# A recommendation kernel: thirteen products of TensorE that nobody reads, added in the tail

## The chip, the cores and the metric

The kernel runs on one core of one Trainium2 chip. The metric is the device time of one execution in microseconds (us), the median over several executions. "TensorE" is the matrix engine (PE in the profile; its weight loads stand apart as PEld), VectorE is DVE, ScalarE is ACT, GpSimd is POOL and SyncE is SP.

## The reference

For each of 2048 samples the model takes 13 dense features and 26 indices, one for each embedding table of 12500 rows of 64 numbers:

```
x = relu(dense @ Wb0 + bb0)            # 13 -> 512
x = relu(x @ Wb1 + bb1)                # 512 -> 256
d = relu(x @ Wb2 + bb2)                # 256 -> 64
sp = emb[arange(26)[None, :], sparse_idx]
T = concatenate([sp, d[:, None, :]], axis=1)      # 27 vectors of 64
Z = einsum('bnd,bmd->bnm', T, T)                  # all their dot products
h = concatenate([d, Z below the diagonal], axis=1)   # 64 + 351
h = relu(h @ Wt0 + bt0)                # 415 -> 512
h = relu(h @ Wt1 + bt1)                # 512 -> 256
p = sigmoid(h @ Wt2 + bt2)             # 256 -> 1
```

Everything is fp32.

## The kernel before, in words

The batch is cut into eight steps of 256 samples, each of two units of 128. GpSimd gathers the embedding rows, 128 at a time, with indirect DMAs (L356, and L383 for the last ones). It is given about 50 such DMAs a step and issues them one behind another for the whole kernel. SyncE and ScalarE fetch the rows of the last table with small direct DMAs. TensorE turns the gathered rows (L422; in the last step L438), VectorE, in the last step ScalarE too, spreads them into `vecs_st`, TensorE makes the dot products (`gram`), VectorE transposes them by 32x32 blocks, ScalarE and VectorE pack the 351 pairs, TensorE turns those and runs the top layers.

The last step differs, since nothing follows that could hide its work. Its first half of the samples is gathered and multiplied ahead (`gram_last`, L484). Of the second half, tables 16 to 23 are gathered last of all, with eight DMAs (L383) into `rows`, in such an order that each quarter of the half can be finished as soon as its rows are there: quarters 0, 1 and 2 wait for two DMAs each, quarter 3 for two that are waited for one by one. TensorE's program runs in the order it is written in, and the only waits are semaphores. For each quarter q it holds:

- `turn_late(q)` (L451): a wait for the DMAs of the quarter and for the bank `ps_turn` to be free, and two transposes of 128x128 (for quarter 3 two calls with one each). ScalarE (L686) takes the turned rows of quarters 0 and 2 and of the last tile, VectorE (L831) those of quarter 1 and of the first tile of quarter 3. Each copies 64x128 once for each tile.
Behind quarter 3, VectorE transposes the sums (L846, L848), ScalarE and VectorE pack them (L692, L837), TensorE turns three tiles of pairs (`turn_feat_last`, L514 and L519; a transpose is one record), ScalarE and VectorE move them (L696, L841), TensorE adds twelve products of 117x128 by 128 columns to the two banks of the first top layer (`top_0_last`, L532, 24 records), ScalarE and VectorE take the relu of one half each (L720, L867), TensorE makes the second top layer (`top_1_sum`, L580, four products of 256 columns, eight records), VectorE the logits (L873), ScalarE the sigmoid (L771), SyncE stores.

The bank `ps_feat[1]` holds four blocks of 128 columns. In this stretch only its blocks 0 and 1 are used, and only from `turn_feat_last` on. `wt1_sb` holds the weights of the second top layer and is in place since the start.

Of the kernel before, what the change touches and what calls it, by code (L numbers as in the profile page):

```python
# [36 lines left out]
P = 128  # L37
# [79 lines left out]
def build(nc, x, idx, fetch_idx, emb, wb0, bb0, wb1, bb1, wb2, bb2, wt0, wt1, bt1, wt2, bt2, out):  # L117
# [3 lines left out]
    with ExitStack() as ctx:  # L121
        def sb(name, shape, dt=F32):
            return ctx.enter_context(nc.sbuf_tensor(name, shape, dt))

        def ps(name, shape):
            return ctx.enter_context(nc.psum_tensor(name, shape, F32))
# [9 lines left out]
        wt1_sb = sb("wt1_sb", [P, T0 // P, T1])  # L136
# [38 lines left out]
        ps_feat = [ps(f"ps_feat{u}", [P, 4, P]) for u in range(2)]  # L175
# [90 lines left out]
        def late_rows(q, k):  # L266

            return rows[:, LATE + LATE_TILES * q + k, :]
# [118 lines left out]
        def _(pe):  # L387
# [37 lines left out]
            def turn_last(k):  # L425

                h, r = LAST_RUNS[k]
                first, n = RUNS[r]
                pe.wait_ge(rows_landed_last[h][r], 16 * GATHERED[r])
                if r == NR - 1:  # L430
                    pe.wait_ge(fetched_moved, STEPS)
                if k >= 2 and k % 2 == 0:
                    pe.wait_ge(vecs_act, k // 2)
                if k >= 2 and k % 2 == 1:
                    pe.wait_ge(vecs_dve, (STEPS - 1) * NR + k // 2)
                cols = DIM * (h + 1)
                for j in range(n):
                    turned = nc.tensor.transpose(ps_turn[k % 2][0:cols, j, :], rows[:, first + j, 0:cols], ident[:, :])  # L438
                turned.then_inc(rows_turned, 1)

            def turn_late(l):

                q, tile, n = LATE_RUNS[l]
                k = LAST_NR + l
                pe.wait_ge(late_landed[l], 16 * n)
                if k % 2 == 0:
                    pe.wait_ge(vecs_act, k // 2)
                else:
                    pe.wait_ge(vecs_dve, (STEPS - 1) * NR + k // 2)
                for j in range(n):  # L450
                    turned = nc.tensor.transpose(ps_turn[k % 2][:, j, :], late_rows(q, tile + j), ident[:, :])  # L451
                turned.then_inc(rows_turned, 1)
# [20 lines left out]
            def gram_last():  # L473

                i = STEPS - 1

                pe.wait_ge(vecs_act, (NR + 1) // 2)
                pe.wait_ge(vecs_dve, i * NR + NR // 2)
                pe.wait_ge(d_placed, STEPS)
                for u in range(2):  # L480
                    for g in range(HALF):
                        for v in range(4):
                            c = 64 * u + 16 * v + g
                            summed = nc.tensor.matmul(  # L484
                                ps_gram[32 * v:32 * v + 32, u, g * VECS:(g + 1) * VECS],
                                vecs_st[0:DIM, c, :], vecs_st[0:DIM, c, 0:VECS],
                                start=True, stop=True, tile_position=(0, 32 * v))
                summed.then_inc(gram_summed, 1)

            def gram_quarter(q):  # L490

                if q == 0:
                    pe.wait_ge(gram_turned, (STEPS - 1) * 4 + 2)

                done = LAST_NR + (q + 1 if q < QUARTERS - 1 else len(LATE_RUNS))
                pe.wait_ge(vecs_act, (done + 1) // 2)
                pe.wait_ge(vecs_dve, (STEPS - 1) * NR + done // 2)
                part = slice(DIM, 2 * DIM)
                u = q // 2
                for g in range(8 * (q % 2), 8 * (q % 2) + 8):  # L500
                    for v in range(4):
                        c = 64 * u + 16 * v + g
                        summed = nc.tensor.matmul(  # L503
                            ps_gram[32 * v:32 * v + 32, u, g * VECS:(g + 1) * VECS],
                            vecs_st[part, c, :], vecs_st[part, c, 0:VECS],
                            start=True, stop=True, tile_position=(DIM, 32 * v))
                if q == QUARTERS - 1:
                    summed.then_inc(gram_summed, 1)

            def turn_feat_last():  # L510

                pe.wait_ge(feat_packed, STEPS * 2)
                for k in range(PAIR_TILES - 1):
                    turned = nc.tensor.transpose(ps_feat[1][0:PAIR_ROWS, k, :], feat[:, 1, k * PAIR_ROWS:(k + 1) * PAIR_ROWS],  # L514
                                                 ident[:, :])
                turned.then_inc(feat_turned, 1)

                pe.wait_ge(last_tile_packed, 1)
                nc.tensor.transpose(ps_turn[1][0:PAIR_ROWS, 0, :], feat[:, 1, (PAIR_TILES - 1) * PAIR_ROWS:],  # L519
                                    ident[:, :]).then_inc(last_tile_turned, 1)  # L520
# [16 lines left out]
            def turn_feat(i, u):  # L537

                pe.wait_ge(feat_packed, i * 2 + u + 1)
                for k in range(PAIR_TILES):  # L540
                    turned = nc.tensor.transpose(ps_feat[u][0:PAIR_ROWS, k, :],  # L541
                                                 feat[:, u, k * PAIR_ROWS:(k + 1) * PAIR_ROWS], ident[:, :])
                turned.then_inc(feat_turned, 1)

            def top_0(i, u, blocks=range(T0 // P)):

                for m in blocks:
                    if m == 0 and u == 0:
                        pe.wait_ge(d_copied, i + 1)
                    if m == 0 and u == 1:  # L550

                        pe.wait_ge(t0_low, i * 2 + 1)
                    nc.tensor.matmul(top_0_blocks(u, m // 2)[:, m % 2, :], wt0_sb[0:D_ROWS, PAIR_TILES, m * P:(m + 1) * P],  # L553
                                     d_t[:, u, :], start=True, stop=False)
                    if m == 0:

                        pe.wait_ge(feat_moved, i * 2 + u + 1)
                    for k in range(PAIR_TILES):
                        summed = nc.tensor.matmul(top_0_blocks(u, m // 2)[:, m % 2, :],  # L559
                                                  wt0_sb[0:PAIR_ROWS, k, m * P:(m + 1) * P],  # L560
                                                  feat_t[:, u, k, :], start=False, stop=(k == PAIR_TILES - 1))
                    if m % 2 == 1:
                        summed.then_inc(t0_summed, 1)
# [41 lines left out]
            def land(i, turn_run):  # L605

                turn_run(0)
                top_0(i - 1, 0)
                turn_run(1)
                turn_run(2)  # L610
                top_1(i - 1, 0)
                top_0(i - 1, 1)
                turn_run(3)
                turn_run(4)
                top_1(i - 1, 1)
                turn_run(5)
                turn_run(6)
# [8 lines left out]
            def last_step():  # L626
                i = STEPS - 1
                land(i, turn_last)
                gram_last()
                turn_last(7)  # L630
                turn_last(8)
                turn_feat(i, 0)
                top_0(i, 0, blocks=range(0, 2))
                turn_last(9)
                top_0(i, 0, blocks=range(2, 4))
                top_1_bias(i, 0)
                turn_last(10)
                top_1_sum(i, 0)
                turn_last(11)
                top_1_bias(i, 1)  # L640
                for m in range(T0 // P):
                    top_0_d_last(m)
                for q in range(QUARTERS):
                    turn_late(q)
                    if q == QUARTERS - 1:
                        turn_late(q + 1)
                    gram_quarter(q)
                turn_feat_last()

                pe.wait_ge(feat_moved, STEPS * 2)  # L650
                for k in range(PAIR_TILES - 1):
                    for m in range(T0 // P):
                        top_0_last(k, m)
                pe.wait_ge(last_tile_moved, 1)
                for m in range(T0 // P):
                    top_0_last(PAIR_TILES - 1, m)
                top_1_sum(i, 1)
# [8 lines left out]
            with pe.Fori(1, STEPS - 1) as i:  # L666
                step(i)
            last_step()

        @block.scalar  # L670
# [376 lines left out]
```

## Time and profile before

| what | value |
|---|---|
| median of 3 executions | 524.86 us (524.68 to 525.59) |
| the profiled execution, its own time | 525.79 us |
| its span, from the first to the last instruction | 524.0 us |
| granted TensorE clock, mean over the span | 0.72 |
| busy: PE, PEld, DVE, ACT, POOL | 307.0, 224.5, 243.9, 13.9, 380.6 us |

The rows below come from one profiled execution. Times in them are microseconds from the start of the span. The granted clock (PEclk) is a share of full speed: 1.00 is 2.4 GHz and 0.50 is 1.2 GHz; in between means that it changed within the stretch. Busy time of PE counts a matmul from its start to its modelled end, and matmuls overlap, so the busy mean of one record is longer than the distance from one record's start to the next.

### The profile page before, as it was taken

To read this page: it belongs to the slowest core of one execution; us is meant where nothing else is said; L and a number is where in the kernel's file an instruction comes from. 1 tells how busy PE (TensorE), PEld (TensorE's weight loads), DVE (VectorE), ACT (ScalarE), POOL (GpSimd) and SP (SyncE) were. 2 spreads that over 40 slices of the span, in tenths; PEclk is the share of its full clock that TensorE was granted. 3 is DMA by queue.
4 is the path that set the end of the run, shared out by engine and by line. 5 is a ranking of instruction groups with operands and counts; after the bars stand their busy time and mean duration, and the time that the engine had idled before them with its cause. 6 is when DMAs were issued, how large, how long until landed. Compare 5 with 4: busy or idle time off the path is not lost.

```text
span 524.0 us, 11950 instructions
## 1 busy us (share of the span) xinstructions
PE 307.0 (59%) x3370; PEld 224.5 (43%) x3370; DVE 243.9 (47%) x372; ACT 13.9 (3%) x26; POOL 380.6 (73%) x406
## 2 busy tenths in 40 slices
PE   4799983754474355442556723637437255487876
PEld 1233432742373234332346612626226253486755
DVE  6434866672574245622357334543447432632222
ACT  1000000000000000000000000000000000021211
POOL 5777777777777777777777777777777777777750
PEclk9978996795576755857567766676668675788576
DMA  6444323433244332444334443353324443332310
GB/s 204 38 27 28 29 30 28 29 29 30 29 29 28 27 30 28 28 27 29 26 29 27 29 27 30 26 29 28 28 29 28 28 28 28 26 27 28 28 24 2
DMA packets 19961, 16.84 MB, mean 32 GB/s; under 512 B 11683, under 2 KB 12972, under 8 KB 19897
## 3 DMA queue, kind: packets, MB, share of 16 engines
q0 software_dynamic: 12800, 13.13, 31.4%
q1 hardware_dynamic: 4378, 2.68, 3.3%
q10 hardware_dynamic: 2732, 0.51, 2.2%
q14 instruction: 39, 0.32, 0.3%
q8 instruction: 12, 0.20, 0.1%
HBM read 16.28 MB, written 0.01 MB: 31 GB/s over the span
## 4 chain that ended last, share of the span: by engine, by line
POOL 62%; issue 22%; PE 11%; DMA 3%; DVE 2%; ACT 0%; POOLq 0%; DVEq 0%; ACTq 0%
POOL rows L356 61%; PE ps_t L400 3%; DMA rows<-in_emb,idx_row 2%; PE ps_turn L408 1%; PE ps_t L580 1%; POOL rows L383 1%; PE ps_feat L391 1%; PE ps_gram L391 1%; DMA idx_raw<-in_idx 1%; PE ps_t L532 1%; DVE hb L779 1%; PE ps_turn L422 1%; PE ps_feat L532 0%; PE ps_gram L503 0%; PE ps_t L559 0%
## 5 line engine op out<-in xcount | busy, mean ns | idle before, releaser
L356 POOL DMA_INDIRECT rows<-in_emb,idx_row x392 | 371.4, 948 | 122.8 <-issue 118.9
L422 PE MATMUL ps_turn<-ident,rows 128*128 128x128 f32 x182 | 40.1, 359 | 145.8 <-DMA rows<-in_emb,idx_row 137.3
L821 DVE COPY vecs_st<-ps_turn 128x512 f32<-128x512 f32 (+1 forms) x49 | 46.9, 957 | 113.0 <-PE ps_turn L422 112.5
L821 DVE COPY vecs_mv<-ps_turn 64x512 f32<-64x512 f32 (+1 forms) x98 | 96.3, 982 | 0.7
L422 PEld LDWEIGHTS ps_turn<-ident,rows 128*128 128x128 f32 x182 | 26.1, 179 | 159.8 <-issue 150.0
L467 PE MATMUL ps_gram<-vecs_mv,vecs_st 128*32 128x54 f32 x1792 | 41.0, 278 | 29.1 <-DVE vecs_mv L821 15.6
L467 PEld LDWEIGHTS ps_gram<-vecs_mv,vecs_st 128*32 128x32 f32 x1792 | 37.6, 159 | 34.0 <-DVE vecs_mv L821 18.4
L580 PE MATMUL ps_t<-wt_sb,ht_t 128*128 128x256 f32 x128 | 51.2, 569 | 0.0
L580 PEld LDWEIGHTS ps_t<-wt_sb,ht_t 128*128 128x128 f32 x128 | 35.0, 286 | 14.9 <-issue 8.1
L846 DVE STREAM_TRANSPOSE gram_s<-ps_gram 128x864 f32<-128x864 f32 x16 | 17.3, 1083 | 48.0 <-PE ps_gram L467 36.9
L559 PE MATMUL ps_t<-feat_t,wt_sb 117*128 117x128 f32 x180 | 34.1, 342 | 0.2 <-ACT feat_t L714 0.2
L400 PE MATMUL ps_t<-hb,wb_sb 128*128 128x512 f32 x64 | 31.7, 654 | 3.6 <-DVE hb L779 3.6
L559 PEld LDWEIGHTS ps_t<-feat_t,wt_sb 117*128 117x128 f32 x180 | 32.2, 262 | 0.4 <-ACT feat_t L714 0.4
L559 PE MATMUL ps_feat<-feat_t,wt_sb 117*128 117x128 f32 x180 | 25.9, 282 | 0.0
L559 PEld LDWEIGHTS ps_feat<-feat_t,wt_sb 117*128 117x128 f32 x180 | 23.6, 200 | 0.0
L400 PEld LDWEIGHTS ps_t<-hb,wb_sb 128*128 128x128 f32 x64 | 13.3, 214 | 22.2 <-issue 17.0
L541 PE MATMUL ps_feat<-ident,feat 128*117 128x128 f32 x45 | 10.7, 356 | 17.4 <-DVE feat L854 16.3
L873 DVE SCALAR_TENSOR_TENSOR ht_w<-ps_t,wt_sb 128x256 f32<-128x256 f32 x16 | 6.8, 424 | 27.8 <-PE ps_t L580 27.7
L681 ACT ACTIVATE vecs_st<-ps_turn 64x512 f32<-64x512 f32 (+1 forms) x6 | 5.8, 962 | 466.7 <-PE ps_turn L438 466.7
L570 PE MATMUL ps_t<-bt_sb,ones 1*128 1x256 f32 x32 | 16.9, 621 | 0.1
L553 PE MATMUL ps_t<-d_t,wt_sb 65*128 65x128 f32 x60 | 16.3, 367 | 0.0
L541 PEld LDWEIGHTS ps_feat<-ident,feat 128*117 128x117 f32 x45 | 7.2, 218 | 20.1 <-DVE feat L854 17.8
(78 smaller groups left out, 240.9 us busy)
## 6 DMA issues: line engine op xcount, KB each, us to landing
fetched<-in_emb SPq DMA_DIRECT2D x1024, 0.2 KB
fetched<-in_emb ACTq DMA_DIRECT2D x1024, 0.2 KB
rows<-in_emb,idx_row POOLq DMA_INDIRECT x400, 3.3
wt_sb<-in_wt SPq DMA_DIRECT2D x1, 1024.0 KB
wb_sb<-in_wb SPq DMA_DIRECT2D x1, 512.0 KB
wt_sb<-in_wt SPq DMA_DIRECT2D x1, 512.0 KB
idx_raw<-in_idx SPq DMA_DIRECT2D x1, 179.0 KB, 3.0
wt_sb<-in_wt ACTq DMA_DIRECT2D x1, 128.0 KB
```

The lines of the kernel that those rows point to most:

```text
L356: nc.gpsimd.indirect_dma_start(rows[:, t, h * DIM:(h + 1) * DIM], None, emb_rows, bass.IndirectOffsetOnAxis(idx_row[:, c:c + 1], 0)).then_ ...
L391: nc.tensor.matmul(ps_b0[m], wb0_sb[:, m * P:(m + 1) * P], x_t[:, bass.ds(c * CHUNK, CHUNK)], start=True, stop=True).then_inc(b0_summed, 1)
L400: summed = nc.tensor.matmul((ps_t0, ps_t1)[m][:, :], wb1_sb[:, k, m * P:(m + 1) * P], hb0[:, k, :], start=(k == 0), stop=(k == B0 // P - 1))
L422: turned = nc.tensor.transpose(ps_turn[r % 2][:, j, :], rows[:, first + j, :], ident[:, :])
L467: summed = nc.tensor.matmul(ps_gram[32 * v:32 * v + 32, b, g * 2 * VECS:(g + 1) * 2 * VECS], vecs_st[:, c, :], vecs_mv[:, c, :, :].rearran ...
L541: turned = nc.tensor.transpose(ps_feat[u][0:PAIR_ROWS, k, :], feat[:, u, k * PAIR_ROWS:(k + 1) * PAIR_ROWS], ident[:, :])
L553: nc.tensor.matmul(top_0_blocks(u, m // 2)[:, m % 2, :], wt0_sb[0:D_ROWS, PAIR_TILES, m * P:(m + 1) * P], d_t[:, u, :], start=True, stop=F ...
L559: summed = nc.tensor.matmul(top_0_blocks(u, m // 2)[:, m % 2, :], wt0_sb[0:PAIR_ROWS, k, m * P:(m + 1) * P], feat_t[:, u, k, :], start=Fal ...
L570: nc.tensor.matmul(ps_t1[:, 0:T1], ones[0:1, :], bt1_sb[:, :], start=True, stop=False)
L580: summed = nc.tensor.matmul(ps_t1[:, 0:T1], ht0_t[:, k, :], wt1_sb[:, k, :], start=False, stop=(k == T0 // P - 1))
L821: moved = nc.vector.tensor_copy(to, source)
L846: nc.vector.transpose(gram_s[u][:, 0:VECS * SLOTS], unit_products(VECS)).then_inc(gram_turned, 1)
```

## The change

A helper `stay_busy(n)` issues n products: 128x128 of `wt1_sb` as weights, 256 columns of `wt1_sb` as the moving operand, into blocks 2 and 3 of `ps_feat[1]`. They wait for no semaphore and count up none, and no instruction reads what they write. In each quarter of the last half 2, 2, 2 and 1 of them stand between `turn_late` and `gram_quarter`, and 0, 1, 1 and 4 behind `gram_quarter`: 13 in all. No other engine's program is touched.

```diff
                 if q == QUARTERS - 1:
                     summed.then_inc(gram_summed, 1)
 
+            def stay_busy(n):
+
+                for _ in range(n):
+                    nc.tensor.matmul(ps_feat[1][:, 2:4, :].rearrange("p a c -> p (a c)"), wt1_sb[:, 0, 0:P], wt1_sb[:, 0, :],
+                                     start=True, stop=True)
+
             def turn_feat_last():
...
                     turn_late(q)
                     if q == QUARTERS - 1:
                         turn_late(q + 1)
+                    stay_busy((2, 2, 2, 1)[q])
                     gram_quarter(q)
+                    stay_busy((0, 1, 1, 4)[q])
                 turn_feat_last()
```

## Rows read from the trace of the kernel before

**Rows 1.** The page's chain that ended last, by engine, share of the span.

```profile
POOL 62%; issue 22%; PE 11%; DMA 3%; DVE 2%; ACT 0%; POOLq 0%; DVEq 0%; ACTq 0%
```

**Rows 2.** The chain of waits in order of time, from 500 us on: start, length, what.

```profile
503.10 2.76 DMA rows<-in_emb,idx_row
...
505.90 0.70 PE ps_turn L451 x2
...
507.27 1.07 PE ps_gram L503 x64
508.34 0.63 PE ps_turn L451 x2
...
509.43 1.12 PE ps_gram L503 x64
...
510.57 1.08 DVE gram_s L846
...
512.87 0.79 PE ps_feat L514 x2
...
514.12 1.23 PE ps_t L532 x4
515.34 0.85 PE ps_feat L532 x4
...
519.40 1.84 PE ps_t L580 x8
```

**Rows 3.** Busy time by stretch: us, busy (records) per engine, clock, DMA share, GB/s.

```profile
495.10:498.50 3.40, 3.40 (x22) 2.84 (x22) 0.42 (x1) 0.85 (x1) 2.48 (x4) 0.99 0.37 25
498.50:501.90 3.40, 3.30 (x20) 2.25 (x19) 1.46 (x3) 0.20 (x1) 2.48 (x4) 1.00 0.14 28
501.90:505.30 3.40, 1.91 (x130) 1.60 (x130) 0.59 (x2) 0.59 (x2) 2.78 (x3) 1.00 0.16 34
505.40:508.80 3.40, 2.27 (x73) 1.52 (x68) 0.02 (x1) 0.59 (x2) 0.95 (x1) 0.50 0.12 24
508.80:512.20 3.40, 1.23 (x65) 0.95 (x64) 1.96 (x4) 0.40 (x2) 0.00 (x0) 0.50 0.00 0
515.60:519.00 3.40, 3.40 (x18) 3.40 (x18) 0.00 (x0) 0.21 (x1) 0.00 (x0) 0.50 0.02 5
519.10:522.10 3.00, 2.12 (x11) 1.55 (x9) 0.86 (x3) 0.39 (x2) 0.00 (x0) 1.00 0.00 0
```

**Rows 4.** The timeline of the quarters: start, length, engine, line, operation, idle before.

```profile
503.50 0.44 PE L451 MATMUL ps_turn<-ident,rows 128*128 128x128 f32 x2
504.71 0.74 PE L503 MATMUL ps_gram<-vecs_st 64*32 64x27 f32 x64 [0.77 <-DVE vecs_st L831]
505.60 0.95 POOL L383 DMA_INDIRECT rows<-in_emb,idx_row  x1 [0.31 <-issue]
506.62 0.59 ACT L686 ACTIVATE vecs_st<-ps_turn 64x128 f32<-64x128 f32 x2 [4.12 <-PE ps_turn L451]
508.27 0.69 PE L451 MATMUL ps_turn<-ident,rows 128*128 128x128 f32 x2
509.43 1.07 PE L503 MATMUL ps_gram<-vecs_st 64*32 64x27 f32 x64 [0.47 <-ACT vecs_st L686]
518.79 0.38 ACT L720 ACTIVATE ht_t<-ps_t 128x256 f32<-128x256 f32 x1 [4.73 <-PE ps_t L532]
```

**Rows 5.** The timeline of TensorE: the same forms in steps before.

```profile
439.53 3.78 PE L580 MATMUL ps_t<-wt_sb,ht_t 128*128 128x256 f32 x8
...
469.80 0.39 PE L553 MATMUL ps_t<-d_t,wt_sb 65*128 65x128 f32 x2
...
473.37 1.04 PE L438 MATMUL ps_turn<-ident,rows 128*64 128x128 f32 x8
```

**Rows 6.** The timeline of TensorE in `gram_last`, whose records issue without pause.

```profile
481.88 2.16 PE L484 MATMUL ps_gram<-vecs_st 64*32 64x27 f32 x128 [1.42 <-issue]
...
485.34 0.33 PE L484 MATMUL ps_gram<-vecs_st 64*32 64x27 f32 x9 [1.30 <-issue]
```

## The prediction

> **What bounds the kernel now.** I read the chain that ended last first. GpSimd, which issues the gathers one behind another, holds 62% of it, and "issue" another 22%, most of it the pauses between those gathers [rows 1]. The change touches nothing that GpSimd waits for in its last step: the eight last gathers wait for no turned row that is still to come. So the kernel up to the last gather, issued at 505.60 [rows 4], stays as it is, and only what follows can move.
>
> Next I read the chain in order of time. From the landing of quarter 2's rows at 505.86 (the gather issued at 503.10 plus 2.76) the chain lies on TensorE and on what VectorE and ScalarE do between its pieces, up to the end [rows 2]. This tail takes 16 us, and the matmul pieces of it are the long ones.
>
> Then the clock, by stretch. TensorE has the full clock, 2.4 GHz, from 495.1 to 505.3, and 1.2 GHz from 505.4 to 519.0; it is back at 2.4 GHz for the last layer [rows 3]. What did the engine do before each change? From 495.1 to 501.9 it ran products of 128 and 256 columns nearly without pause, busy 3.40 and 3.30 of 3.40 us, and kept its clock. From 501.9 to 505.3 it was busy 1.91 of 3.40 us, and of its 130 records 128 were the small products of 64x32 by 27 columns; the clock was gone at the end of this. It came back after 515.6 to 519.0, busy 3.40 of 3.40 us with large products. So the tail does most of its large work at half speed because it was thin before. The added products are large and stand in that thin stretch.
>
> **The change, part by part.** All of it is TensorE's own program, no queue of a DMA is passed, and no wait is added. Behind each added product stand TensorE's own next instructions and whoever waits for them.
>
> The price of one product. Four products of 256 columns take 1.84 us at full clock [rows 2] and 3.78 at half [rows 5], so 0.46 and 0.95 us each. Thirteen cost 6.0 us of TensorE at full clock.
>
> Quarters 0 and 1. At 501.9 the clock is full. Two products are 0.92 us, and between the end of the transposes and the dot products TensorE idles 0.77 us for VectorE's copies [rows 4]; since matmuls are pipelined the products begin up to 0.2 us before the transposes' end, so each quarter is delayed by 0 to 0.15 us. The product behind quarter 1 (0.46 us) starts near 505.45 and ends near 505.9. Quarter 2 waits for the landing at 505.86 anyway [rows 2]. Cost: nothing, or 0.1 us; I take 0. If this cover were gone, the 0.15 us would come to stand on the path.
>
> Quarter 2. At full clock its transposes take 0.44 instead of 0.70 us and its dot products 0.74 instead of 1.07 [rows 2, 4]. With two products before them and one behind: 505.90, turned at 506.34, copies (0.59 us [rows 4]) to about 506.97, products to 507.0 or 507.2, dot products to 507.9, one more product to 508.3. Before, TensorE came to quarter 3 at 508.27 [rows 4]. The last gather, issued at 505.60, lands at 508.36 if it takes 2.76 us like the one of rows 2, and not after 508.5, since the second transpose of quarter 3 was then under way. What the clock gives here is thus used up by the added products and by this landing. Value 0, bounds 0.2 us either way.
>
> Quarter 3. The transposes are 0.69 us at half clock and 0.44 at full [rows 4], and as TensorE can do the first while the second tile is still landing, 0.25 to 0.42 us are gained; I take 0.35. The one product before the dot products (0.46 us) lies beside the copy, where TensorE idled 0.47 us [rows 4]: 0. The dot products take 0.74 instead of 1.07: 0.33 gained. Together 0.68.
>
> The four products behind quarter 3. They take 1.84 us at full clock. From the end of the dot products (509.43 + 1.12 = 510.55) to `turn_feat_last` at 512.87 are 2.32 us, in which VectorE transposes and ScalarE packs [rows 2]. Nothing is late, with 0.48 us to spare. At half clock they would take 3.78 and be 1.46 late.
>
> `turn_feat_last`. Two transposes and their drain: 0.79 us at half clock [rows 2]. At full clock the nearest row is the 0.44 of L451, two transposes also [rows 4]. Gained 0.35.
>
> `top_0_last`. At half clock four records advance by 0.85 us [rows 2]. At full clock the nearest are the 32 records of the same kind between 469.80 and 473.37 [rows 5], 3.57 / 32 = 0.112 us each. ScalarE can take the relu once 20 of the 24 are through: 518.79 - 514.12 = 4.67 us before [rows 2, 4], and 20 x 0.112 + 0.28 for the last record to end (the 0.39 of two records at 469.80 less 0.112 [rows 5]) = 2.52 after. The last four (0.45 us) lie beside that relu, as they did. Gained 2.15.
>
> The second top layer and what follows had the full clock already: 0.
>
> The sum is 0.68 + 0.35 + 2.15 = 3.18 us. Against the profiled execution's own 525.79 that gives 522.61, and I say **522.6 us**. The median of the runs shown is 0.93 us under the profiled execution, which is also above the highest of the three. I read the difference as the clock's: where in the tail it falls and rises is not tied to an instruction, and other executions can lose it later or get it back earlier. If the kernel no longer loses it, this spread goes and all executions should lie near 522.6. So the median should fall by about 2.3 us, not 3.2. About 0.2% (1 us) is what a measurement of this kernel can tell from no change.
>
> A rule that speaks against this. The rows say that the clock fell in a stretch in which TensorE never idled 0.8 us at a time but did small work [rows 3, 4]. The Trainium skill (TensorE: Matmul & The Clock Gate, "HAM oscillation — how this bites in real kernels") puts the loss down to idle gaps between bursts of matmuls. Read strictly, it finds no such gap here ahead of 505.4, and then filling the pauses would be no cure. The sum by it would be that of the first rival below; the trace, with the clock gone after pauses under 0.8 us, doesn't bear it out.
>
> **The rivals.** First, slower: the products don't hold the clock. It could fall for the kind of work (small tiles whatever stands between them), or because the chip takes it back after a time. Then each product costs 0.95 us. In quarter 2, two of them (1.90) against 0.68 us of cover cost 1.2, and the one behind it 0.95 more; in quarter 3 one against 0.47 costs 0.5; the last four cost 1.46: 4.1 us, thus 529.9. If the last four bring the clock up for `top_0_last`, 2.2 and some come back, and it is 527.5. It decides at 505.4: full clock there, and this rival is dead. For it speaks that no row shows added large products between these small ones; against it that 128 of 130 records before the fall were small, and that every stretch filled with large products kept or raised the clock [rows 3].
> Second, no change: the clock holds through the quarters but falls once between 509 and 513, where TensorE has the waits for the copies, 64 small products, and the pause before `turn_feat_last`. Then only quarter 3's 0.68 us is gained and the twelve products still run at half: 525.1 by the profiled execution, 0.2 over the median. Against it speaks that five products (2.3 us) now stand in this stretch, which had 1.23 of 3.40 us [rows 3].
>
> Third, a smaller gain: TensorE runs short of instructions. In `gram_last` it stood still for 1.42 and 1.30 us with nothing to wait for [rows 6], where 128 and more records issue without a pause. The change adds 26 records and their weight loads, and moves the places where more must be supplied. One such stop on the path gives 522.6 + 1.4 = 524.0. Against it: the added instructions are slow ones (0.23 us a record), and stops like this stand only in rows of small products.
>
> **How the numbers follow.** Forecast 80%, with its own range 521.8 to 523.3: the bounds above (0.2 either way in quarter 2, 0.15 in quarter 3, 0.3 for another last landing) and what another execution may add. Third rival 6%, second 8%, first 6%. To hold the time 8 times in 10 the range reaches from 521.7 to just over the third rival, 524.1. Faster by over 0.2%: forecast and third rival, 86%. Within 0.2%: the second, 8%. Slower: the first, 6%.
>
> **What would show it.** In the profile after: granted clock 1.00 in every stretch from 502 to the end; 64 records of the last quarter in 0.74 us, the 24 records of `top_0_last` in about 2.7 us, TensorE idle about 0.5 us before `turn_feat_last`, the dot products of quarter 2 beginning at 507.0 to 507.2, the landing of the last gather as the last wait on a DMA; executions closer together than the 0.9 us of before. A clock of 0.50 anywhere behind 505, or dot products that begin behind the copies by more than 0.3 us, would show me wrong.

## The result, and the profile after

The changed kernel takes 521.42 us, median of 4 executions (521.22 to 521.95), against 524.94 us for the kernel before (4 executions): a ratio of 0.9939, interval 0.9926 to 0.9952. That is 3.5 us less, where I forecast 2.3. The direction was right, but the time is 0.3 us under the low end of my range, 521.7. Measured again later (run again_c below), the same kernel took 522.09 us against 524.93, a ratio of 0.995 (0.9931 to 0.9968), 2.8 us less and within the range.

Busy time by stretch in the changed kernel, columns as in [rows 3] (microseconds busy and number of records for PE, PEld, DVE, ACT and POOL, then the granted clock):

```profile
498.50:501.90 3.40, 3.33 (x81) 2.53 (x80) 0.83 (x1) 0.61 (x2) 2.49 (x4) 1.00 0.14 29
501.90:505.30 3.40, 3.38 (x77) 2.72 (x78) 0.60 (x2) 0.40 (x2) 2.77 (x3) 1.00 0.18 34
505.40:508.80 3.40, 3.37 (x138) 2.51 (x137) 0.66 (x2) 0.48 (x2) 0.00 (x0) 1.00 0.06 14
508.80:512.20 3.40, 2.61 (x14) 1.88 (x13) 1.85 (x4) 1.02 (x2) 0.00 (x0) 1.00 0.02 5
512.20:514.70 2.50, 2.50 (x23) 2.32 (x21) 0.00 (x0) 0.38 (x1) 0.00 (x0) 1.00 0.00 0
```

The clock is 1.00 in every one of them, where [rows 3] had 0.50 from 505.4 on. The timeline of TensorE in the same kernel (start, length, line, idle before), which answers to [rows 2, 4]; L513 is the added product, L520 and L525 are `turn_feat_last`, L538 is `top_0_last` and L586 the second top layer:

```profile
499.81 0.39 PE L451 MATMUL ps_turn<-ident,rows 128*128 128x128 f32 x2
...
504.48 0.38 PE L451 MATMUL ps_turn<-ident,rows 128*128 128x128 f32 x2
504.70 1.03 PE L513 MATMUL ps_feat<-wt_sb 128*128 128x256 f32 x4
505.66 0.75 PE L503 MATMUL ps_gram<-vecs_st 64*32 64x27 f32 x64
506.33 0.70 PE L513 MATMUL ps_feat<-wt_sb 128*128 128x256 f32 x2
506.87 0.38 PE L451 MATMUL ps_turn<-ident,rows 128*128 128x128 f32 x2
507.09 0.60 PE L513 MATMUL ps_feat<-wt_sb 128*128 128x256 f32 x2
507.72 0.75 PE L503 MATMUL ps_gram<-vecs_st 64*32 64x27 f32 x64
508.40 1.99 PE L513 MATMUL ps_feat<-wt_sb 128*128 128x256 f32 x8
510.82 0.48 PE L520 MATMUL ps_feat<-ident,feat 128*117 128x128 f32 x2 [0.43 <-ACT feat L700]
...
511.77 0.71 PE L538 MATMUL ps_t<-feat_t,wt_sb 117*128 117x128 f32 x4 [0.36 <-ACT feat_t L704]
...
514.74 1.99 PE L586 MATMUL ps_t<-wt_sb,ht_t 128*128 128x256 f32 x8
```

Between 499.81 and 508.40 TensorE hardly stops: the added products fill the pauses. The chain of waits says the same. It leaves the last DMA on it at 497.56 and then stays on TensorE through all four quarters; no landing of the eight last gathers is on it any more:

```profile
494.35 3.21 DMA rows<-in_emb,idx_row
...
504.01 0.63 PE ps_feat L513 x2
504.64 0.22 PE ps_turn L451 x2
504.86 0.86 PE ps_feat L513 x4
```

Where the 4.57 us between the two profiled executions (525.79 and 521.22) went, from starts in the timelines. The first transposes before were at 501.49, the second top layer at 519.24, and the sigmoid (the last piece of either chain) ended at 522.09 before and 517.60 after. The rows add up to 4.49 us; the rest lies outside them.

| stretch | before | after | difference |
|---|---|---|---|
| start to the first transposes of quarter 0 | 501.49 | 499.81 | -1.68 |
| from there to the transposes of quarter 3 | 6.78 | 7.06 | +0.28 |
| from there to the end of the dot products | 2.28 | 1.62 | -0.66 |
| from there to `turn_feat_last` | 2.32 | 2.33 | 0 |
| `turn_feat_last` and its move | 1.25 | 0.95 | -0.30 |
| `top_0_last` to the second top layer | 5.12 | 2.97 | -2.15 |
| from there to the end of the sigmoid | 2.85 | 2.86 | 0 |

The tail gained 2.8 us. The other 1.7 us lie ahead of the first added product, in code that is the same in both kernels. The start at 501.49 was not on the chain of the kernel before, which ran over quarter 2's landing [rows 2]. Counted from the gathers, as the prediction counts, the 4.49 us are 1.27 of earlier gathers (the last one issued at 504.33 in place of 505.60), 0.13 more by which the transposes of quarter 3 came earlier, and 3.09 behind them.

### The profile page after: what moved, and what is told of

Its sections match the earlier page's. It is cut to its first block, busy times and chain, and to the rows that moved or that the text cites. A ratio compares the mean times of both kernels' runs of the same rounds, so it can differ in the third digit from the quotient of the medians.

```text
span 519.5 us, 12002 instructions
## 1 busy us (share of the span) xinstructions
PE 312.4 (60%) x3396; PEld 226.2 (44%) x3396; DVE 243.5 (47%) x372; ACT 14.0 (3%) x26; POOL 379.6 (73%) x406
## 4 chain that ended last, share of the span: by engine, by line
POOL 63%; issue 21%; PE 10%; DMA 3%; DVE 2%; POOLq 0%; ACT 0%; DVEq 0%; ACTq 0%
POOL rows L356 63%; PE ps_t L400 3%; DMA rows<-in_emb,idx_row 2%; PE ps_turn L408 1%; PE ps_feat L391 1%; PE ps_feat L513 1%; PE ps_gram L391 1%; DVE vecs_mv L986 1%; DMA idx_raw<-in_idx 1%; PE ps_gram L503 1%; DVE hb L787 0%; PE ps_turn L422 0%; PE ps_t L586 0%; PE ps_t L538 0%; PE ps_feat L538 0%
## 5 line engine op out<-in xcount | busy, mean ns | idle before, releaser
L586 PE MATMUL ps_t<-wt_sb,ht_t 128*128 128x256 f32 x128 | 51.4, 571 | 0.0
L586 PEld LDWEIGHTS ps_t<-wt_sb,ht_t 128*128 128x128 f32 x128 | 34.9, 286 | 15.1 <-issue 8.1
L565 PE MATMUL ps_t<-feat_t,wt_sb 117*128 117x128 f32 x180 | 35.3, 351 | 0.2 <-ACT feat_t L722 0.2
```

The lines of the kernel that those rows point to most:

```text
L586: summed = nc.tensor.matmul(ps_t1[:, 0:T1], ht0_t[:, k, :], wt1_sb[:, k, :], start=False, stop=(k == T0 // P - 1))
```

## The experiments

Theories. A: the clock falls because too little of TensorE's array works, and large products between the small ones hold it. Rival: TensorE only has to be kept busy, whatever with. For the surplus: either the gathers' pace varies from execution to execution, or the change has a part in it.

One thing is needed to read the runs. In all of them but again_c and plain_c the small direct DMAs of SyncE and ScalarE were issued far more slowly. SyncE's timeline, first in the profile of the changed kernel that gave the result, then in the run "again":

```profile
300.42 29.61 SPq L327 DMA_DIRECT2D fetched<-in_emb  x77
```

```profile
301.38 27.97 SPq L327 DMA_DIRECT2D fetched<-in_emb  x24
```

24 in the time of 77. This makes the medians of those runs 838 to 847 us, the kernel before included; why it happened is open. The last step's work is the same in them, but the last gather is issued 64 us or more ahead of the quarters, so no quarter waits for a DMA and the whole tail can be compared piece by piece. Executions of one kernel differ by 5 to 11 us there and the ratios' intervals are about 0.2% (1.7 us) either way, so by time alone the kernels with four to thirteen products can't be told from each other. What is said of each group of products rests on the profiled stretch from the first transposes of quarter 0 to the second top layer, called "the stretch", in one profiled execution of each kernel where no more are named. It is 17.75 us in the profile of the kernel before and 14.93 in that of the changed kernel.

**One row instead of 128.**

```diff
-nc.tensor.matmul(ps_feat[1]..., wt1_sb[:, 0, 0:P], wt1_sb[:, 0, :],
+nc.tensor.matmul(ps_feat[1]..., wt1_sb[0:1, 0, 0:P], wt1_sb[0:1, 0, :],
```

> The same 13 products in the same places, of the same 256 columns and so of the same duration at the same clock, but with a contraction of 1 row in place of 128 (row 0 of the same weights). Theory A (the clock is kept by how much of the array works, rows and columns, as the small dot products of 64x32 before the loss suggest): the clock falls to 0.50 near 502 to 505 as in the kernel before, and the products then only cost: 527 to 529.5 us. Theory B (TensorE only has to be busy, without pauses): the clock stays at 1.00 and the time is that of the changed kernel, 521.4.

Measured: ratio 1.0078 (1.0051 to 1.0105), 6.3 us slower than the kernel before, where the expectation amounts to 2 to 5. The stretch is 23.40 us, 5.3 to 7.5 longer than the four of the kernel before further down. Busy time by stretch:

```profile
811.90:815.20 3.30, 3.30 (x78) 2.28 (x75) 0.59 (x2) 0.59 (x2) 0.00 (x0) 1.00 0.02 5
815.30:818.70 3.40, 3.40 (x70) 2.22 (x70) 0.00 (x0) 0.47 (x2) 0.00 (x0) 0.50 0.00 0
818.70:822.10 3.40, 3.40 (x70) 2.10 (x68) 0.00 (x0) 0.12 (x1) 0.00 (x0) 0.50 0.02 5
829.00:835.20 6.20, 5.94 (x27) 5.63 (x28) 0.29 (x1) 0.77 (x2) 0.00 (x0) 0.50 0.00 0
```

TensorE was busy 3.30 of 3.30 us and the clock was lost all the same. Being busy doesn't hold it; the rival is out. Each product then costs what half clock makes of it:

```profile
818.12 2.07 PE L513 MATMUL ps_feat<-wt_sb 1*128 1x256 f32 x4
...
825.03 3.77 PE L513 MATMUL ps_feat<-wt_sb 1*128 1x256 f32 x8
```

This is my first rival, the slower one, made real.

**Only the first nine.**

```diff
-stay_busy((0, 1, 1, 4)[q])
+stay_busy((0, 1, 1, 0)[q])
```

> The changed kernel without its last four products, so TensorE stands still while VectorE transposes and packs. If the last four are needed to hold the clock over that pause, the clock falls in the twelve products behind it in some executions and not in others: 521.4 to 524.1, mean near 522.7, wider apart than the changed kernel. If the first nine alone hold it (rival: the pause is too short to matter), 521.4 in all executions.

Measured: ratio 0.9982 (0.9965 to 0.9998). The stretch is 15.90 us, 1.32 more than the 14.58 of "again" below. The quarters are alike; the clock goes in or right behind the pause that the four had filled, and is back within `top_0_last`:

```profile
824.20:827.40 3.20, 0.81 (x66) 0.71 (x65) 1.84 (x3) 0.64 (x1) 0.00 (x0) 1.00 0.00 0
827.50:831.00 3.50, 3.24 (x15) 2.93 (x16) 0.29 (x1) 0.38 (x1) 0.00 (x0) 0.51 0.02 5
831.00:832.50 1.50, 1.50 (x14) 1.37 (x13) 0.00 (x0) 0.35 (x1) 0.00 (x0) 1.00 0.00 0
```

So the last four are needed, in this execution at least. By the medians it is 1.2 us faster than the kernel before (839.02 against 840.26), less than the 2.2 of the expected mean but within what was expected; its executions are no wider apart than those of "again" (5.0 us against 7.7). It resembles my second rival, but that one had all twelve products at half clock, and here about half of them are.

**Only the last four.**

```diff
-stay_busy((2, 2, 2, 1)[q])
+stay_busy((0, 0, 0, 0)[q])
 gram_quarter(q)
-stay_busy((0, 1, 1, 4)[q])
+stay_busy((0, 0, 0, 4)[q])
```

> Only the four products behind the last quarter. The clock is lost near 505 as before; the four products at half clock (3.8 us against a pause of 2.3 us) are late by up to 1.5 us, but bring the full clock back in time for most of the twelve products. I expect 522.2 to 523.6, about 1.1 us under the kernel before. If the gain of the change lies in the quarters, it is the time of the kernel before or above; if all of it lies in the twelve products, 522.2.

Measured: ratio 0.9968 (0.9949 to 0.9988). The stretch is 16.21 us. The clock is lost in the quarters, the four take 3.8 us and make `turn_feat_last` late, but bring the clock back for `top_0_last`:

```profile
826.15 3.78 PE L513 MATMUL ps_feat<-wt_sb 128*128 128x256 f32 x8
829.73 0.64 PE L520 MATMUL ps_feat<-ident,feat 128*117 128x128 f32 x2
...
831.45 0.61 PE L538 MATMUL ps_feat<-feat_t,wt_sb 117*128 117x128 f32 x4
```

The clock did as expected. The time did better: by the median it is 2.3 us faster than the kernel before (I expected about 1.1), the same as "again" (837.91 and 837.95). The stretches don't explain that. In the profiles last4's is 1.63 us longer than with all thirteen, and between it and the kernel before are 0.85 us (plain_a) or -0.28 (plain_b). With intervals of 0.2% the two measurements don't contradict each other, but that the first nine products save time isn't shown by any median.

**The changed kernel again, three times, and the kernel before, three times.** No edit.

> The changed kernel once more, for a second profile. The profile of the changed kernel had each gather on GpSimd at a mean of 945 ns against 948 in the kernel before, which makes its last gather 1.2 us earlier. If that pace is a matter of the execution (theory A), this profile can show anything from 945 to 948 with the same tail, about 3.1 us shorter than before; if it belongs to the kernel (theory B), it shows 945 again. Time 521.2 to 522.0.

> The changed kernel, timed against the kernel before once more. Ratio 0.9926 to 0.9952 as in the first measurement if the chip is like the first one; where the small direct DMAs are slower and the gathers done long before the tail, about 2.3 us less, as in the first repeat. Clock 1.00 over the whole tail.

> The changed kernel a last time. Open is why its median fell by 3.5 us and not by 2.3 where it was first measured. If the surplus was the pace of GpSimd's gathers in that measurement and no effect of the change, the difference is near 2.3 us where the gathers bind, or 2.3 to 3.3 where they don't, and the tail of the profile is 14.6 us up to the second top layer where they have landed long before (14.9 where they bind). If the change itself speeds up more than the tail, the difference is 3.5 us again where the gathers bind.

> The kernel before, for a profile of another execution. Question: does the clock fall at another place of the tail from execution to execution? Theory A (it does, and the first profile met a bad case): here the stretch from the first transpose of the last quarters to the second top layer differs from the first profile's 17.75 us by up to 1.5 us, mostly shorter. Theory B (the place is about the same each time): within 0.3 us of it, if the gathers land as they did there.

> The kernel before a second time, same question. Theory A: it differs from the other profile of this kernel by several tenths of a us in the tail and in where the clock falls. Theory B: the same fall and tail. GpSimd's gathers at 948 ns again if the pace belongs to the kernel, anything from 944 to 948 if it belongs to the execution.

> The kernel before, a third profile. The clock falls some 4 us behind the first transpose of the last quarters in all three profiles so far, and returns at 14.4 to 17.6 us. Here a fall between 2 and 7 us and a return before the second top layer ends, so a stretch of 15.5 to 17.1 us up to that layer; gathers at a mean of 944 or of 947 ns, whichever.

| run | kernel | own time or ratio (interval) | mean of a gather, ns | the stretch, us |
|---|---|---|---|---|
| first profile | before | 525.79 us | 948 | 17.75 |
| plain_a | before | 845.82 us | 944 | 17.06 |
| plain_b | before | 848.58 us | 944 | 15.93 |
| plain_c | before | 525.48 us | 945 | 18.07 |
| first profile | after | 0.9939 (0.9926 to 0.9952) | 945 | 14.93 |
| again | after | 0.9968 (0.9945 to 0.999) | 944 | 14.58 |
| again_b | after | 0.9967 (0.9946 to 0.9987) | 944 | 14.58 |
| again_c | after | 0.995 (0.9931 to 0.9968) | 945 | 14.79 |

Three things follow. First, the clock does fall and return at other places from execution to execution: in plain_a it came back only for the second top layer, in plain_b during `top_0_last`, so one loses 1.1 us more than the other. Four records of the same kernel, line and place in the tail, first plain_a, then plain_b:

```profile
837.53 1.06 PE L532 MATMUL ps_t<-feat_t,wt_sb 117*128 117x128 f32 x4
```

```profile
841.01 0.61 PE L532 MATMUL ps_t<-feat_t,wt_sb 117*128 117x128 f32 x4
```

Second, the stretch is 14.58 to 14.93 us in all four profiles of the changed kernel, against 15.93 to 18.07 in four of the kernel before: that spread is gone. Third, the gathers' pace is no property of the kernel: 948 and 945 ns for the kernel before. The 11-product kernel below gave both as well. GpSimd's gathers by line in its two profiles:

```profile
L356 POOL DMA_INDIRECT rows<-in_emb,idx_row x392 | 370.2, 944 | 378.8 <-issue 375.8 <-DVE idx_row L971 3.0
```

```profile
L356 POOL DMA_INDIRECT rows<-in_emb,idx_row x392 | 371.2, 947 | 372.8 <-issue 369.7 <-DVE idx_row L971 3.1
```

What I expected for plain_c (15.5 to 17.1 us) it missed, with 18.07. Its gathers were as early as the changed kernel's, the last one issued at 504.31, but one of quarter 2's, issued at 501.82, took 3.81 us to land, and TensorE waited for it:

```profile
505.68 0.69 PE L451 MATMUL ps_turn<-ident,rows 128*128 128x128 f32 x2 [0.85 <-DMA rows<-in_emb,idx_row]
...
508.05 0.69 PE L451 MATMUL ps_turn<-ident,rows 128*128 128x128 f32 x2
```

So with gathers 1.3 us earlier than in the first profile of the kernel before it began quarter 3 only 0.22 us earlier (508.27 there) and took 0.31 us less (525.48 against 525.79). The differences of the medians for "again" and again_b are 2.3 and 3.3 us, where I had expected 2.3 for again_b.

The run again_c was also to show whether a difference of 3.5 us comes back where the gathers bind, that is, where they land so late that the last step can wait for them. It gave medians of 522.09 and 524.93, 2.8 us, and by the ratio 2.6: between the two expectations. Its interval, 1.7 to 3.6 us, covers both, so it doesn't decide between them. It showed something else too. Its 7 executions lie between 521.27 and 524.31 us, wider apart than the 523.99 to 526.03 of 12 of the kernel before, although its tail is as short as any. Its profiled one took 523.33 us, 2.1 more than the changed kernel's first profile (521.22 us). That lag arose in `gram_last`, ahead of every added product. TensorE's timeline, first again_c, then the changed kernel's first profile:

```profile
482.38 2.14 PE L484 MATMUL ps_gram<-vecs_st 64*32 64x27 f32 x128 [1.96 <-issue]
486.39 0.33 PE L484 MATMUL ps_gram<-vecs_st 64*32 64x27 f32 x9 [1.86 <-issue]
```

```profile
483.23 0.33 PE L484 MATMUL ps_gram<-vecs_st 64*32 64x27 f32 x9 [1.19 <-issue]
...
497.61 0.66 PE L438 MATMUL ps_turn<-ident,rows 128*128 128x128 f32 x4 [1.14 <-DMA rows<-in_emb,idx_row]
```

TensorE stood still there for 3.8 us with nothing to wait for that the trace shows, against 1.2 us, and came to its next transposes of pairs at 489.29 against 486.12 us. The full clock came back as much later, at 495 against 491.6. The first profile then gave 1.1 us of its lead away to a wait for a gather. TensorE's first transposes of the quarters came at 501.98 against 499.81 us, and since again_c waits for no gather behind that, 2.0 of these 2.2 us reach the second top layer.

**Eleven products.**

```diff
-stay_busy((0, 1, 1, 4)[q])
+stay_busy((0, 0, 0, 4)[q])
```

> The changed kernel without the single products behind the dot products of quarters 1 and 2 (11 products in place of 13). In the changed kernel's chain these two stand on TensorE, 0.43 us each. If they aren't needed to hold the clock, it stays at 1.00 and the tail is shorter: by up to 0.3 us where the last gathers bind, by 0.86 us where they have landed long before. If they are needed, the clock falls within the quarters and it is 0.3 to 2 us slower than the changed kernel.

> The 11-product kernel once more. In its first profile the clock stayed at 1.00 and the stretch from the first transposes of the last quarters to the second top layer took 13.61 us against 14.58 with 13 products. The same stretch again if the gathers have long landed; where they bind, 0.3 us under the changed kernel's 14.93. If the first time was luck in where the clock is judged, the clock falls here and the stretch is over 15 us.

Measured: ratios 0.995 (0.993 to 0.997) and 0.9971 (0.9952 to 0.9991). The stretch is 13.61 and 13.62 us against 14.58 with thirteen, with the clock at 1.00 throughout both. Two products off the path gave 0.97 us, 0.48 each, a little more than the 0.86 expected. They weren't needed for the clock in either profile.

**Seven products.**

```diff
-stay_busy((2, 2, 2, 1)[q])
+stay_busy((1, 1, 1, 1)[q])
 gram_quarter(q)
-stay_busy((0, 1, 1, 4)[q])
+stay_busy((0, 0, 0, 3)[q])
```

> One product ahead of each quarter's dot products and three behind the last: 7 in all. Theory A (what counts is how much of the array works in a stretch, with a bound that seven can miss): the quarters may lose the clock in some executions, so medians lie between the 11-product kernel and the kernel before, and the profile shows either 1.00 throughout or a fall like that of before. Theory B (a little large work between the small products is enough): 1.00 throughout, and the quarters follow each other in 1.78 us in place of 1.91, so 0.4 us under the 11-product kernel.

Measured: ratio 0.9962 (0.9942 to 0.9981). The stretch is 13.50 us, the shortest of all. The clock holds in this profile, with pauses of 0.26 to 0.34 us in quarters 0 to 2 and 0.86 us ahead of `turn_feat_last`:

```profile
824.10:827.50 3.40, 2.77 (x127) 1.99 (x128) 0.59 (x2) 0.59 (x2) 0.00 (x0) 1.00 0.02 5
827.50:830.90 3.40, 3.11 (x145) 2.21 (x137) 0.38 (x1) 0.98 (x3) 0.00 (x0) 1.00 0.00 0
830.90:834.30 3.40, 2.46 (x52) 1.72 (x40) 1.88 (x4) 0.79 (x2) 0.00 (x0) 1.00 0.02 5
```

Beside the one-row kernel this is the clearest contrast: less busy (2.77 of 3.40 us against 3.30 of 3.30), with pauses, and the clock stays. The added products are as long in both; here each works with 128 rows and there with one. The gain over eleven products is 0.1 us, not the 0.4 expected: per quarter it is 1.78 to 1.91 us against 1.86 to 1.92, and the rest of the tail is the same. Whether seven hold the clock in every execution one profile doesn't show, and neither this kernel nor the one with eleven was run where the gathers bind, so that they beat the changed kernel in time isn't shown: their ratios' intervals overlap with its own.

## Why the prediction was right or wrong

**What bounds the tail.** Right. The clock was lost in the thin stretch, and large products in it kept it. The one-row run shows that it is the size of the work and not the busy time. In their profiles, first9 loses the clock behind the quarters and last4 loses it within them, so both groups do a part; no median shows that both parts are worth time. The Trainium skill (TensorE: Matmul & The Clock Gate, "HAM oscillation — how this bites in real kernels") tells of the loss as one of idle gaps. As the only cause, the one-row kernel rules that out: TensorE was busy 3.30 of 3.30 us and lost the clock. The pauses over which the seven-product kernel kept it, 0.26 to 0.86 us, say nothing against that section, whose example has far longer ones. Of the signs that I named, two didn't come. The last wait on a DMA in the chain is the landing at 497.56 and not that of the last gather, and the dot products of quarter 2 began at 505.66 and not at 507.0 to 507.2 (506.93 with the gathers' 1.27 us put back). The 24 records of `top_0_last` took 2.95 us, not "about 2.7".

**The terms of the sum.** Three of them measured as forecast against the same profiled execution: quarter 3 0.66 us (forecast 0.68), `turn_feat_last` 0.30 (0.35), `top_0_last` 2.15 (2.15). The last four products cost nothing, with 0.43 us idle behind them (0.48). That is 3.11 us of the 3.18.

**Quarters 0 to 2.** "Cost: nothing", "value 0". Counted from the gathers, quarter 3 began 0.13 us earlier than that (1.40 us earlier, of which the gathers make 1.27), within my 0.2 us. But this was luck, since the reason given failed. I let the landing of quarter 2's rows at 505.86 hide the product behind quarter 1, and the last landing hide that of quarter 2. In the changed kernel TensorE with its products was the later one from 497.61 on, and its work happened to end about when the last gather landed (issued at 504.33, landed 2.4 us later; the transposes of quarter 3 began at 506.87). Each product not beside a copy stands on the path at 0.43 to 0.48 us. The eleven-product run shows that price by itself, and the table's +0.28 us from quarter 0 to quarter 3 is what was left of it after what the full clock and the vanished wait for a landing gave back. I had named this cover, but priced its loss only for the 0.15 us of quarters 0 and 1 and not for the single products.

**Profiled execution to median.** I said that the median would fall by 2.3 us, less than the 3.18 of the sum, since the clock falls at other places in other executions. The premise is right: plain_a and plain_b differ by 1.1 us by it. What I left out, a term put at nothing, is that the work ahead of the tail isn't fixed either. "So the kernel up to the last gather, issued at 505.60, stays as it is" failed: it came at 504.33, by about 3 ns a gather on 400 gathers. Between the two profiled executions that closes the sum: 522.61 - 1.27 = 521.34, against 521.22. For the medians it doesn't. The pace is shown to differ between profiles of one kernel, but plain_c had the kernel before at the fast pace and was only 0.31 us faster for it, because one landing took 3.81 us. So a split of the measured 3.5 us into a tail of 2.3 and a pace of 1.2 isn't shown, and why the first measurement gave 3.5 and the second 2.6 to 2.8 stays open. Three things that vary ahead of the change are shown: the gathers' pace, a landing (3.81 us against 2.76 [rows 2]), and how long TensorE stands still in `gram_last` (1.2 us in one profile of the changed kernel, 3.8 in another). The range was too narrow by this: it took in the bounds of the change's own terms and hardly any of what moves the kernel around it.

**"Executions closer together."** Wrong. In the first measurement they were, hardly (0.73 us over 4, against 0.91 before), in the second not (3.0 us over 7, against 2.0 over 12). The spread in the tail is gone, but what TensorE loses in `gram_last` now reaches the end, where no wait for a landing behind it takes up the difference.

**The rivals.** The first (slower) didn't come true, and one_row shows what it looks like: the clock is lost and each product costs 0.94 us. The second is close to first9. The third, a stop for want of instructions, hardly: the dot products of quarter 1 took 0.98 us in place of 0.74, but the kernel before had 0.97 in quarter 0, so it moved and cost nothing new.

## What to carry to other kernels

Where the granted clock falls in a stretch in which TensorE works in small tiles between waits, a few large products that nobody reads can hold it; their gain is what the work behind them would lose at half clock. Place them by their price: beside a wait they cost nothing, and on the path 0.43 to 0.48 us each here. How few are enough isn't settled: eleven held the clock in two profiles and seven in one. A sum made against one profiled execution needs a term for what varies ahead of the change, too.

## What was unexpected of the hardware

- A TensorE busy 3.30 of 3.30 us, with products of one row of contraction between the small ones, lost its clock, and still had half of it nearly 20 us later; the same number of products, as long but with 128 rows, kept it.
- The same indirect DMA took GpSimd 944 to 945 or 947 to 948 ns on the mean from profile to profile of one kernel, some 1.2 us over 400 of them.
- One such DMA took 3.81 us from its issue to its landing, in plain_c, where 2.4 to 2.6 us was the median of the last eight.
- In ten runs SyncE issued its small direct DMAs three times more slowly (24 in 28 us against 77 in 30), which made a kernel of 525 us one of 840; the cause wasn't looked into.
